# The last router of a four-layer kernel fed with the residual sums instead of scaled rows

## The reference, cut to what matters

```python
x = x + o @ w_up                      # o: output of the attention
res = x
t = _rmsnorm(x, g2).reshape(-1, D)    # x * g2 * rsqrt(mean(x*x) + EPS)
probs = jax.nn.softmax(t @ router_w, axis=-1)
vals, idx = jax.lax.top_k(probs, 2)
w = vals / jnp.sum(vals, axis=-1, keepdims=True)
# per token: silu(t @ w1[e]) * (t @ w3[e]) @ w2[e], weighted by w, for its two experts
return res + y
```

## Time and profile before

| | us |
|---|---|
| median of 3 runs | 3182.34 (3182.22 to 3183.45) |
| profiled execution | 3179.92 |
| its span | 3178.6 |
| last head's end to first product of the counts (2869.5 to 2898.15) | 28.6 |
| routed chunks, first transposes to last product (2920.4 to 3152.1) | 231.7 |

### The profile page before, as it was taken

How to read it: one execution, slowest core, us unless ns; L and a number is a source line. 1 busy time by engine, 2 the same in 40 slices (tenths; PEclk the granted TensorE clock), 3 DMA queues, 4 the chain that set the end, 5 groups by cost and what they waited for, 6 DMA issues and landing times.

```text
span 3178.6 us, 43530 instructions
## 1 busy us (share of the span) xinstructions
PE 3011.6 (95%) x16332; PEld 2211.4 (70%) x16332; DVE 2116.0 (67%) x3869; ACT 1225.1 (39%) x2357; POOL 859.9 (27%) x1308
## 2 busy tenths in 40 slices
PE   8999999999999999999999999899999899997996
PEld 6778777677767776777699999665567655555664
DVE  7996788558855885686478887783328677764113
ACT  5343333552354335432233333441225356662331
POOL 3207301100100020001246556440433231112554
PEclk9999999999999999999999999999999999998998
DMA  7000100010002000200032222003650011113533
GB/s 192 15 1 1 56 1 1 14 60 10 0 14 69 1 1 14 68 1 1 14 91 83 80 80 67 21 1 106 225 190 1 30 34 46 33 38 123 204 125 109
DMA packets 104614, 176.42 MB, mean 56 GB/s; under 512 B 27125, under 2 KB 75799, under 8 KB 99671
## 3 DMA queue, kind: packets, MB, share of 16 engines
q1 hardware_dynamic: 89527, 102.32, 10.5%
q0 software_dynamic: 14880, 71.33, 6.4%
HBM read 198.31 MB, written 17.56 MB: 68 GB/s over the span
## 4 chain that ended last, share of the span: by engine, by line
PE 75%; DVE 14%; issue 4%; ACT 2%; DMA 2%; POOL 1%; SPq 1%; DVEq 0%; ACTq 0%; POOLq 0%
PE psum L424 9%; PE psum L447 8%; PE psum L1444 7%; PE psum L1456 6%; PE psum L2578 6%; PE psum L1925 5%; PE psum L1880 5%; PE psum L2599 3%; PE psum L1164 2%; PE psum L414 2%; PE psum L460 2%; PE psum L2754 2%; PE psum L3179 2%; DVE psum L3437 1%; PE psum L3199 1%
## 5 line engine op out<-in xcount | busy, mean ns | idle before, releaser
L424 PE MATMUL psum<-Vt,shared 128*128 128x256 f32 (+1 forms) x1600 | 362.1, 381 | 0.4
L447 PE MATMUL psum<-Kt,xnTt 128*128 128x512 f32 (+1 forms) x960 | 343.8, 508 | 0.6 <-ACT xnTt L537 0.6
L424 PEld LDWEIGHTS psum<-Vt,shared 128*128 128x128 f32 (+1 forms) x1600 | 298.1, 190 | 39.6 <-issue 1.5
L447 PEld LDWEIGHTS psum<-Kt,xnTt 128*128 128x128 f32 x960 | 179.9, 190 | 158.0 <-issue 154.1
L245 POOL TENSOR_SCALAR root_v<-meanvar 128x8 f32<-128x8 f32 (+3 forms) x19 | 8.6, 454 | 904.2 <-DVE meanvar L223 904.2
L1456 PEld LDWEIGHTS psum<-expert_w,prep 128*128 128x128 f32 x1024 | 194.6, 190 | 77.7 <-issue 57.4
L3437 DVE CUSTOM_DVE_ANT_0 psum<-psum,expert_w 128x128 f32<-128x128 f32 (+7 forms) x256 | 191.8, 775 | 76.6 <-PE psum L3179 73.5
L1456 PE MATMUL psum<-expert_w,prep 128*128 128x256 f32 x1024 | 240.8, 379 | 0.0
L1444 PE MATMUL psum<-weights,expert_w 128*128 128x512 f32 x512 | 240.3, 593 | 0.0
L1370 DVE SCALAR_TENSOR_TENSOR bias<-Kt,small,bias 128x1232 f32<-128x1232 f32 x96 | 149.1, 1554 | 129.8 <-ACT Kt L1354 128.5
L3326 ACT ACTIVATE prep<-psum 128x512 f32<-128x512 f32 (+3 forms) x384 | 167.3, 494 | 108.7 <-PE psum L3202 107.8
(11 more groups left out here) (516 smaller groups left out, 6691.8 us busy)
## 6 DMA issues: line engine op xcount, KB each, us to landing
weights<-in_L_ffn_w SPq DMA_DIRECT2D x32, 512.0 KB, 4.8
expert_w<-in_L_ffn_w SPq DMA_DIRECT2D x32, 512.0 KB, 4.7
expert_w<-in_L_xattn_Wf SPq DMA_DIRECT2D x16, 512.0 KB, 5.7
weights<-q_parts SPq DMA_DIRECT2D x32, 144.0 KB
weights<-k_parts SPq DMA_DIRECT2D x96, 48.0 KB
weights<-in_L_xattn_Wk SPq DMA_DIRECT2D x4, 1024.0 KB, 4.9
weights<-in_L_xattn_Wv SPq DMA_DIRECT2D x4, 1024.0 KB, 8.4
weights<-in_L_xattn_Wq SPq DMA_DIRECT2D x4, 1024.0 KB, 5.3
```

The lines of the kernel that those rows point to most:

```text
L424: ins = pe.matmul(o_bank(t), probT[0:rows, t % 2, c, :], Vt[0:rows, t // TB, c, :], start=(c == 8), stop=(c == 7))
L447: ins = pe.matmul(flat[:, par * 3 * BANK + at:par * 3 * BANK + at + cols], xnTt[:, par, k, :], Kt[:, t // TB, k, src:src + cols], start=(k ...
```

## The change

The router of batch 1 takes the sums themselves. G transposes `inner` in place of `send3` (for batch 0 too) and waits for the Y step alone. The logits thus are without the factor of the inverse root, which is the same for all experts of a token and changes no choice. For batch 1, DVE no longer takes `bn_stats`, the aggregate and the scaled rows; ACT does, behind its G copies: eight `Square` activations that sum into `meanvar`, and, after the copy for the counts, eight multiplications into `send3`. The subtraction of the maximum and the exponential ahead of the selection are gone; the two gates come from exp((second - first) * rstd) at the end. The 23 and 14 products of `pe_stay_at_work` become 37 behind the last L.

```diff
         elif kind == "G":
-            pe.wait_ge(rows_ready, NT + TB * b + 2 * i + 2)
+            pe.wait_ge(step_taken, taken(STEP_AT["Y", b, i]))
...
-                                       send3[:, TB * b + 2 * i + t, k * P:(k + 1) * P], ident[:, :])
+                                       inner[:, TB * b + 2 * i + t, k * P:(k + 1) * P], ident[:, :])
...
         for u in range(46, len(LATENT_STEPS)):
-            if u == STEP_AT["G", 1, 0]:
-                pe_stay_at_work(pe, psum[:, 6, :], 23)
             pe_step(pe, u)
-        pe_stay_at_work(pe, psum[:, 7, :], 14)
+        pe_stay_at_work(pe, psum[:, 7, :], 37)
         pe_counts(pe, 1, srow(0, NT * E).rearrange("p (t e) -> p t e", e=E))
...
         for u in range(46, len(LATENT_STEPS)):
             act_step(act, u)
+        act.wait_ge(step_taken, taken(STEP_AT["Y", 1, 3]))
+        for t in range(TB, NT):
+            ins = act.activation(send3[:, t, :], inner[:, t, :], ACT.Square, scale=float(D) ** -0.5,
+                                 accum_out=meanvar[:, t, 1:2])
+        ins.then_inc(variance_made, 1)
+        act_counts(act, 1)
+        act.wait_ge(root_made, ROOTS)
+        for t in range(TB, NT):
+            act.mul(send3[:, t, :], inner[:, t, :], rstd[:, t:t + 1]).then_inc(rows_ready, 1)
+        act_codes(act, 1)
         act.wait_ge(gating_product, 3)
-        act.activation(wide[:, 0], wide[:, 0], ACT.Exp).then_inc(gating_back, 1)
-        act_counts(act, 1)
-        act_codes(act, 1)
+        act.activation(rank[:, :], rank[:, :], ACT.Exp).then_inc(gating_back, 1)
...
             dve.tensor_tensor(pair, bank, pair, ALU.add).then_inc(step_taken, 1)
+            if b == 1:
+                return
...
-        for u in range(46, 52):
-            dve_step_of(dve, u)
-        dve_mean_square(dve, 1)
-        dve.wait_ge(root_made, dve_roots())
-        for i in range(4):
-            dve_sent_rows(dve, 1, i)
-        for u in range(52, len(LATENT_STEPS)):
+        for u in range(46, len(LATENT_STEPS)):
             dve_step_of(dve, u)
         dve.wait_ge(step_taken, taken(len(LATENT_STEPS) - 1))
-        p, first_, second_, left = (wide[:, n] for n in range(4))
-        dve.tensor_reduce(top_a[:, :], logits[:, :, :], AX.X, ALU.max).then_inc(dve_step, 1)
-        dve.wait_ge(dve_step, vs())
-        dve.tensor_tensor(p, logits[:, :, :], over(top_a[:, :]), ALU.subtract).then_inc(gating_product, 1)
-        dve.wait_ge(gating_back, 4)
-        dve_first_best(dve, first_, p, top_a[:, :])
-        dve.scalar_tensor_tensor(left, first_, -2.0, p, ALU.mult, ALU.add).then_inc(dve_step, 1)
+        first_, second_, left = (wide[:, n] for n in range(1, 4))
+        dve_first_best(dve, first_, logits[:, :, :], top_a[:, :])
+        dve.scalar_tensor_tensor(left, first_, -3.0e38, logits[:, :, :], ALU.mult, ALU.add).then_inc(dve_step, 1)
```

More of the change, by code:

```diff
@@ L2286, in build @@
     TOTALS = (23, 39)
+    ROOTS = 69
     WSLOTS = 4
@@ L3491, in dve_latent @@
         dve_tokens(dve, 1)
-        dve.tensor_tensor(rank[:, :], top_a[:, :], top_b[:, :], ALU.add).then_inc(dve_step, 1)
+        dve.tensor_tensor(rank[:, :], top_b[:, :], top_a[:, :], ALU.subtract).then_inc(dve_step, 1)
         dve.wait_ge(dve_step, vs())
[L3494 to L3500, removed]
+        dve.wait_ge(root_made, ROOTS)
+        dve.tensor_tensor(rank[:, :], rank[:, :], rstd[:, :], ALU.mult).then_inc(gating_product, 1)
         for t in range(NT):
@@ L3503, in dve_latent @@
         ins.then_inc(inner_added, 1)
+        dve.wait_ge(gating_back, 4)
+        dve.tensor_scalar(top_a[:, :], rank[:, :], 1.0, None, ALU.add).then_inc(dve_step, 1)
+        dve.wait_ge(dve_step, vs())
+        dve.reciprocal(top_a[:, :], top_a[:, :]).then_inc(dve_step, 1)
+        dve.wait_ge(dve_step, vs())
+        dve.tensor_scalar(gates[:, :, 0], top_a[:, :], tanh_g[:, 7:8], None, ALU.mult).then_inc(dve_step, 1)
+        dve.wait_ge(dve_step, vs())
+        dve.tensor_tensor(gates[:, :, 1], gates[:, :, 0], rank[:, :], ALU.mult).then_inc(dve_step, 1)
+        dve.wait_ge(dve_step, vs())
         dve_routed(dve, 1)
@@ L3625, in pool_latent @@
         pool_root(pool, EPS, TB, NT)
+        assert pool_roots.value == ROOTS
         pool_routed(pool, 1, *L3_rows, a["L3_experts"])
```

## The result

| | before | changed |
|---|---|---|
| median of 19 runs, us | 3177.62 (3172.14 to 3183.45) | 3171.46 (3165.31 to 3179.15) |
| ratio | | 0.9979, 95% interval 0.9972 to 0.9986 |
| profiled execution, us | 3179.92 | 3169.78 |
| its span | 3178.6 | 3168.5 |

The change makes the kernel faster by 0.21%, 6.7 us by the ratio (4.4 to 8.9) and 6.2 by the medians. The forecast was 5.5 us less and a time of 3176.8 in a range from 3172.5 to 3180.5.

The account below looks back on a forecast made before the run. PE was taken to bound the chunks, with a Y, DVE, POOL, DVE, PE, DVE chain before the counts. Gain 6.4 - 0.3 - 0.6 = 5.5 us; 3179.92 - 5.5 = 3174.4, plus 2.4 gives 3176.8 us, range 3172.5 to 3180.5.

Parts of the forecast that it names:

- the last term of the sum: Whole kernel: 2.4 us added to get from the profiled 3179.92 us to the 3182.34 median of runs shown.
- the early fall: G and L steps: clock drops to 1.2 GHz as early as 2878.5, counts at 2893.1, gain 5.0 us.
- both dear bounds: Upper cost bounds: 2 us for the rows' store delaying the weights, 1.7 us for a clock fall where chunks start.
- G no longer waits for the root: Router of batch 1: G starts at about 2875.5, last L ends at 2880.9 at 2.4 GHz, before 2892.95.
- The 37 products are the last to arrive: Between last L and counts: products take 8.3 us at 2.4 GHz, ending 4.2 us behind the selection.
- The clock: G, L and the products: falls at 2880.0, rises 3.0 us into the products; counts at 2891.7, gain 6.4 us.
- Rival A: Router through the products: clock stays at 2.4 GHz, counts at 2889.2, gain 8.0 us, time 3174.3 us; chance 0.25.
- ACT at nothing: ACT's added squares and multiplications, 0.374 us per square, are hidden behind other work; cost bounds 0 and 0.5 us.
- The store: Scaled rows' store, now issued near POOL's first weights fetch: costs 0.3 us, bounds 0 and 2 us.
- The start of the chunks: PE's idle gap before the first chunk: clock may fall there; 0.6 us loss taken, bounds 0 and 1.7.
- Rivals C and D: C: counts follow selection at 2885.0, 3170.1 us, chance 0.03. D: ACT's squares bind at 2 us each, 3181.1, chance 0.04.
- Rival B: Products: clock falls early, stays low through all 37; counts at 2899.8, 7.4 us slower, 3189.7 us; chance 0.04.

Follow-up runs that it names:

- The experiment: Changed kernel with batch 1's mean squares back on DVE, ACT only scaling the rows; counts 20.0 us behind the last head, first chunk 43.0.

## Why the prediction was right or wrong

*The time.* The step that failed is the last term of the sum: the 2.4 us added to get from the profiled execution to the median of the runs shown, and with it that median, 3182.34, as the time of the kernel before. That median was one of three runs that lay within 1.2 us of each other; I took their agreement for the kernel's spread. Its 19 runs span 11.3 us with a median of 3177.62, below the profiled execution. Without that step the sum gives 3174.4, and from the median of 19 runs 3172.1. The range had no term for it, and the time fell 1.0 us below it; put on the median of 19 runs, 4.7 us lower, the same range goes from 3167.8 to 3175.8 and holds the 3171.46. The profile could have warned: it has stretches at 1.2 GHz ahead of the changed place too, and I priced the clock within that place only.

*The range's own working* has a slip on the other side. A gain of 3.0 us was to be the early fall with both dear bounds, but 5.0 - 2 - 1.7 is 1.3 us, which is 3181.0, above the upper end of 3180.5. It didn't matter for the miss.

*No measurable change at 0.60, faster at 0.36.* The ratio of 0.9979 is at the edge, on the side of faster; by the interval it may be 0.14% as well as 0.28%. The forecast of 5.5 us lies inside the interval of 4.4 to 8.9.

*G no longer waits for the root.* Right. L was to end at 2880.9 at 2.4 GHz, 11.35 us behind the last head; it ended at 11.85 with the clock up and at 12.9 to 13.7 with a fall. The eight steps, put at 5.4 us, thus took 5.9 to 6.0 at 2.4 GHz, 0.5 more than worked out from the third layer.

*The selection* was to take 3.85 us: 3.86 in the changed kernel, from 2875.91 to 2879.77.

*The 37 products are the last to arrive.* Right, in all eight profiles with 37 and the changed router; shown from both sides by 14 in the changed kernel and 37 in the one before. Their price at 2.4 GHz was to be 8.3 us, and 8.2 to 8.3 us it was.

*The clock.* The bounds were the counts at 19.65 (no fall) and 23.55 (early fall) behind the last head; the eight profiles gave 20.05 four times, 21.7 once and 23.2 three times. The level I took, 22.15, is between two clusters that I hadn't seen as such; the mean of the eight is 21.4. Rival A, no fall in or just behind L, had a chance of 0.25 and came in four of eight; it put the counts at 19.65, and they were at 20.05. The rise among the products was to come 3.0 us in, and does so roughly: in the changed kernel PEclk from 2876 to 2885 is 0.86, which puts it at 2878.5, 3.0 us behind 2875.51.

The Trainium skill, "TensorE: Matmul & The Clock Gate", section "Why this matters for your kernels", advises against long idle gaps between bursts. No fall without a gap was weighed as rival A. Between the last head and the counts PE is never idle for more than 0.56 us at a time in the changed kernel, and yet the clock fell in four of the eight profiles and stayed up in four, the changed kernel's own on both sides. To keep gaps short wasn't enough here.

*ACT at nothing.* Right. A square costs 0.40 us with its accumulator read, just over the lower bound of 0.374 taken, and the squares end 9.4 us ahead of the counts. The experiment shows more: the move itself is worth nothing.

*The store,* 0.3 us, was too small, if the store is what delays the rows: their landing took 0.9 us longer in the changed kernel's profile, and 0.6 to 1.0 in most others with 37 products. The first chunk lay 0.8, 0.7 and 0.4 us further behind the counts in the changed kernel's three executions. The reason given, that the weights have slack, misses that the token rows are fetched while the weights' transfer ends: the delay is at the rows' landing.

*The start of the chunks,* 0.6 us: the clock fell there in all three profiles of the changed kernel, and took 1.5 us in the first eight products (5.2 against 3.7). I gave it a third. Up to the end of the span the three took 2.0, 0.2 and 1.9 us more from the first chunk on than the 258.2 of the kernel before.

*The sum.* 6.4 - 0.3 - 0.6 = 5.5 came near the measured 6.7 (4.4 to 8.9) in part by luck, since errors cancel: the counts gained about 7.2 in the mean (28.6 - 21.4), the first chunk's distance took 0.4 to 0.8 and the chunks 0.2 to 2.0.

Rivals C and D are out: nothing in the eight profiles comes near them. Rival B is out too; the clock rose within the 37 products each time.

## What to carry to other kernels

When a wait goes, the products that covered it have to go as well: counted in the engine's own order, cover that outlasts the wait it stands in is work on the path, and here 23 needless products gave back about half of what the change could gain. Price such filler against the end of the wait (here 4.1 us from the last L to the selection's end, against 8.2 us of filler), at both clock levels. And before a forecast in absolute time, look at how far the clock of the unchanged part differs between executions: three runs that agree don't show it.

## What the hardware did that I had not expected

The granted clock is not a property of the kernel. In one and the same code ahead of the last head, executions had it at 1.00 or at 0.52 for the 14 us from 2554 to 2568, and in or just behind the L steps it fell in four of eight profiles. The reading of an accumulator on ScalarE has an instruction of its own of 0.19 us, which overlaps with the next square, so that the pair costs 0.40 us.
